# Transposes of x and o by DMA instead of TensorE, key features in half-height tiles, and a new order of each turn

## What is computed

```
q, k, v = heads(layernorm(x) @ Wq.T + bq), heads(ctx @ Wk.T + bk), heads(ctx @ Wv.T + bv)
qf, kf = relu(q @ Wqf.T), relu(k @ Wkf.T) * mask              # 64 features a head
kv, ksum = sum over keys of kf^T v, sum over keys of kf
x = x + (concat over heads of (qf @ kv) / (qf @ ksum + 1e-8)) @ Wo.T + bo
y = layernorm(x)
a = (quant(y) @ ternary(w_up).T) * relu(quant(y) @ ternary(w_gate).T) ** 2
x = x + quant(subln(a) * subln_weight) @ ternary(w_down).T
```

## Time and profile before

| what | value |
|---|---|
| median of 3 runs | 457.24 us (456.74 to 459.41) |
| profiled execution, its own time | 456.15 us |
| its span | 454.0 us |
| PE / DVE / ACT / POOL busy, share of the span | 90% / 85% / 73% / 32% |
| head | 0 to 31.0 us |
| turns 0, 1, 2, 3 | 63.0, 62.8, 60.9, 50.9 us |
| feed-forward | 185.5 us, from 268.6 us on |
| mean granted TensorE clock | 0.977 of full |

### The profile page before, as it was taken

One profiled execution on the slowest core, in us unless ns is written; L12 is line 12 of the kernel. 1 busy time (PEld: TensorE's weight loads), 2 busy tenths in 40 slices (PEclk: granted clock), 3 DMA queues, 4 the chain that ended last, 5 costly groups with the idle time before them and its releaser, 6 DMA issues. The chain is left out here.

```text
span 454.0 us, 8245 instructions
## 1 busy us (share of the span) xinstructions
PE 409.8 (90%) x2800; PEld 212.0 (47%) x2816; DVE 384.9 (85%) x822; ACT 331.7 (73%) x475; POOL 144.0 (32%) x146
## 2 busy tenths in 40 slices
PE   3997999999799998999994889899999989899955
PEld 1454546575255564455753634344444434344421
DVE  3588696699989998999889867999999999898962
ACT  5388998665667594866767658978788786988870
POOL 1018300046000821002200006646556464655430
PEclk9999999999899999999996799999999999999989
DMA  8899994001321242033111441333334342444234
GB/s 221 289 392 409 338 359 167 1 0 50 139 82 61 93 139 92 0 113 118 48 48 48 150 151 24 58 83 81 82 81 88 77 96 67 100 93 99 69 71 116
DMA packets 59025, 54.38 MB, mean 120 GB/s; under 512 B 45232, under 2 KB 45232, under 8 KB 58864
## 3 DMA queue, kind: packets, MB, share of 16 engines
q1 hardware_dynamic: 58096, 50.55, 36.9%
q0 software_dynamic: 896, 3.41, 2.0%
HBM read 39.27 MB, written 4.19 MB: 96 GB/s over the span
## 5 line engine op out<-in xcount | busy, mean ns | idle before, releaser
L1236 PE MATMUL ps<-tern,xqT 128*128 128x512 bf16 x503 | 112.5, 379 | 2.8 <-PEq L166 1.3
L1056 POOL TENSOR_TENSOR actg<-acts,subln 128x512 f32<-128x512 f32 x64 | 84.5, 1336 | 77.0 <-DVE acts L1139 72.3
L1236 PEld LDWEIGHTS ps<-tern,xqT 128*128 128x128 bf16 x512 | 49.6, 98 | 63.8 <-DVE acts L1139 3.8
L1249 PE MATMUL ps<-tern,aqT 128*128 128x512 bf16 x249 | 59.2, 387 | 12.1 <-DMA aqT<-aq 11.7
L1067 ACT ACTIVATE relu<-ps 128x512 f32<-128x512 f32 x64 | 37.3, 583 | 16.4 <-PE ps L1236 16.4
L1139 DVE TENSOR_TENSOR acts<-relu,ps 128x512 f32<-128x512 f32 x64 | 42.3, 678 | 4.4 <-ACT relu L1071 4.3
L1249 PEld LDWEIGHTS ps<-tern,aqT 128*128 128x128 bf16 x256 | 24.8, 99 | 45.2 <-DMA aqT<-aq 13.0
L1071 ACT ACTIVATE relu<-relu 128x512 f32<-128x512 f32 x64 | 40.3, 630 | 2.0
L537 DVE SCALAR_TENSOR_TENSOR fl<-ps,fh 128x512 f16<-128x512 f32 x64 | 39.6, 679 | 2.5 <-ACT fh L400 2.5
L1144 DVE TENSOR_REDUCE amax<-actg 128x1 f32<-128x1024 f32 x32 | 38.7, 1210 | 1.0 <-POOL actg L1056 0.7
L1078 ACT ACTIVATE square<-acts 128x2048 bf16<-128x2048 f32 x16 | 30.4, 1902 | 12.2 <-DVE acts L1139 12.2
(11 more groups left out here) (164 smaller groups left out, 963.6 us busy)
## 6 DMA issues: line engine op xcount, KB each, us to landing
tern<-in_wffn SPq DMA_DIRECT2D x24, 512.0 KB, 11.4
wst<-in_wffn SPq DMA_DIRECT2D x24, 512.0 KB, 3.2
xs<-in_x SPq DMA_DIRECT2D x4, 1024.0 KB, 7.4
out<-res SPq DMA_DIRECT2D x16, 256.0 KB, 2.2
ctxf<-in_ctxT POOLq DMA_DIRECT2D x3, 1024.0 KB, 10.1
xno<-in_wkT SPq DMA_DIRECT2D x4, 256.0 KB, 5.7
...
```

What stands on the lines that cost most here:

```text
L1056: nc.gpsimd.tensor_tensor(actg[:, s % 2, q], acts[:, s % 2, q], subln[:, q], ALU.mult)\
L1236: mm = nc.tensor.matmul(acc, xqT[:, s % XT, k, :], weights[k][:, 512 * c:512 * c + 512], start=(k == 0), stop=(k == KC - 1))
L1249: mm = nc.tensor.matmul(down_bank(s), aqT[:, s % 2, k, :], down_w[:, k, :], start=(k == 0), stop=(k == FK - 1))
```

## The change

- x and o are no longer transposed by PE. ACT makes the fp16 high half of the [128 x 512] tile (L549 of the changed kernel, L557 for o), POOL the low half beside it (L447, L454), and one DMA transpose on SP's queue turns the 1024 columns into `xT` or `oT` (L343, L350). `xn` is one buffer, `xn2`, `o32` and `o2` are two. ACT's normalising of tile n waits for POOL's low half of tile n-1, and its high half of tile n for the landing of transpose n-2.
- X and T leave `ORDER`, and `ORDER` is rewritten: F0 F1 Q0 F2 ... F7 Q1 Q2 S0 S1 S2 S3 Q3, K and V units spread between R, N and O.
- F uses 64*128 tiles: 96 matmuls of 128 columns a turn, alternating between the upper and the lower 64 rows, with two PSUM banks.
- POOL takes over the low half of kv (L460) and the clipping of the ternary chunks (L468). The context's load moves from POOL's queue to SP's, behind `ctx_split`.
- DVE's pieces for S and N are merged over two banks (fewer, wider instructions).
- The second group of x and its context are issued by SP ahead of the raw chunks; SP issues 6 raw chunks, then the four transposes of turn 0, then the other 18.
- All turns are written out (no hardware loop). `xqb` and `xqT` share the memory of the context.
- The feed-forward part is the same.

```diff
-ORDER = (
-    [("X", 0), ("X", 1)] + [("F", i) for i in range(4)] + [("X", 2), ("X", 3)] + [("F", i) for i in range(4, 8)]
-    + [("Q", 0), ("Q", 1), ("S", 0), ("S", 1), ("Q", 2), ("S", 2), ("S", 3), ("Q", 3)]
-    + [("R", p) for p in range(PAIRS)]
-    + [("K", m) for m in range(KC)]
...
+ORDER = [(u[0], int(u[1:])) for u in (
+    "F0 F1 Q0 F2 F3 F4 F5 F6 F7 Q1 Q2 "
+    "S0 S1 S2 S3 Q3 R0 R1 R2 R3 K0 R4 "
+    "R5 R6 R7 K1 V0 N0 N1 N2 N3 K2 N4 "
+    "N5 N6 N7 V1 V2 K3 O0 V3 O1 O2 O3 "
+).split()]
+ACT_AFTER = {
...
+    ("S", 1): (("norm", 0),),
...
+    ("N", 2): (("chunk", 2),),
+    ("N", 3): (("chunk", 3), ("oh", 0), ("norm", 2)),
...
# sync
+            for c in range(EARLY):
+                raw_chunk(c)
+            for t in range(GT):
+                turn_x(0, t)
+            for c in range(EARLY, NCH):
+                raw_chunk(c)
...
+            def turn_x(o, t):
...
+                if o > 0:
+                    sp.wait_ge(filled["Q"], o * KC)
+                sp.wait_ge(feat_ok, 1)
+                sp.wait_ge(xn_split, n + 1)
+                sp.dma_start_transpose(xT[:, :, t * P:t * P + P], xn2[:, n % 2, :]).then_inc(xT_in[n % 2], 16)
+            def turn_o(o, t):
...
+                sp.wait_ge(o_split, n + 1)
+                sp.dma_start_transpose(oT[:, :, t * P:t * P + P], o2[:, n % 2, :]).then_inc(oT_in[n % 2], 16)
# gpsimd
+                nc.gpsimd.tensor_tensor(xn2[:, n % 2, H:2 * H], xn[:, :], xn2[:, n % 2, 0:H], ALU.subtract)\
+                    .then_inc(xn_split, 1)
...
+                nc.gpsimd.tensor_scalar(ternh[:, c, :], wst[:, c % 2], 2.0, 1.0, ALU.min, ALU.subtract)\
+                    .then_inc(chunk_used, 1)
# scalar
+            def normalise(o, t):
...
+                if n > 0:
+                    act.wait_ge(xn_split, n)
+                nc.scalar.activation(xn[:, :], xs[:, n, :], ACT.Identity, bias=shift[:, t:t + 1],
+                                     scale=rstd[:, t:t + 1]).then_inc(xn_ok, 1)
+                if n > 1:
+                    act.wait_ge(xT_in[n % 2], landed(n - 2))
+                act.wait_ge(xn_ok, n + 1)
+                nc.scalar.activation(xn2[:, n % 2, 0:H], xn[:, :], ACT.Copy).then_inc(xn_high, 1)
# tensor
+                terms = ((qkTh, feath), (qkTl, feath), (qkTh, featl))
+                for c in range(KC):
+                    for n, (k, f) in enumerate(terms):
+                        for h in range(2):
+                            rows = slice(64 * h, 64 * h + 64)
...
+                            mm = nc.tensor.matmul(acc[:, c // 2, c % 2], k[rows, c, t * P:(t + 1) * P],
+                                                  f[rows, 0, P * h:P * h + P], start=(n == 0),
+                                                  stop=(n == len(terms) - 1))
```

783 lines of the change are left out of this document (403 added, 380 removed).

## The result

The changed kernel takes **472.97 us** (median of 4 runs, 470.94 to 477.23), the kernel before, on the same chip, 456.99 (455.45 to 459.41): a ratio of 1.036, 95% interval 1.027 to 1.044. The forecast was 448.2 with a range of 440 to 461, so it had the wrong sign and missed by 25 us. The profiled run took 472.07 us, 1.8 more than its span.

The account below looks back on a forecast made before the run. PE was taken to bind turns 1 and 2, DVE just behind; 454.0 + 13.5 - 9.8 - 7.9 - 4.9 = 444.9 us of span, 447.1 with 2.15 added, 448.2 as median; range 440 to 461.

Parts of the forecast that it names:

- eight clips 8 x 1.3 (L341 doubled): POOL's list in turns 1 and 2: each clip priced at 1.3 us, within 34.3 of 51 us busy.
- second rival: POOL's queue becomes the bound: at 2 us a clip o's later tiles come some 4 us late; 460 us, chance 13%.
- The chunks go round through POOL and back through SP: Turns 1 and 2: chunk 4 can be loaded once POOL has clipped chunk 2 at 29.7; ACT wants it at 34.
- The exclusive lock: VectorE and GpSimd share a pair of ports, locked for a whole instruction; the second rival's price was left as it was.
- Turn 0: the step: Turn 0: Q0 waits for four DMA transposes behind six raw chunks, starting at 50.2 instead of 41.8; 76.5 us, +13.5.
- fourth rival: Turn 0's transposes are not held by the raw chunks, so Q0 starts 7 us earlier; 441 us, chance 17%.
- first rival: F's row halves do not run side by side: +2.5 in turns 1 to 3; 455.7 us, chance 12%.
- third rival: A DMA transpose takes much longer than 3.2 us: gain gone at 5.6 us, 471 us at 8; chance 10%.
- Turns 1 to 3 with the assumed clip: Turns 1 and 2 at 53.0 us each (-9.8 and -7.9), turn 3 at 46 us (-4.9).
- the sum (25.4 to 32): Turn 3: all N done at 25.4, o's chain bare, its first transpose landed at 32, where O0 starts.

Follow-up runs that it names:

- a_clip_fast: The changed kernel with GpSimd's clip made a multiply by 1 and add of -1 over the same 1024 elements, clipping left out; 455.6 us, ratio 0.993 to 0.998.
- a_sign: The changed kernel with no clip on any engine: ScalarE's second pass over a chunk becomes a Sign written straight to bf16; 455.0 us, ratio 0.994 to 0.998.

## Why the prediction was wrong, point by point

- **The step that failed: "eight clips 8 x 1.3 (L341 doubled)".** L341 is a multiply and add of 512 elements, 658 ns. The clip is a min and subtract, and takes 3.66 us; multiply and add of 1024 takes 1.04. The same form of instruction on the same engine with other operations differs by 3.5 times. No row of before showed POOL doing a min or a scalar subtract; the price was taken from a row with the right form and the wrong operations. The runs showed in its place 29 us of clips a turn on POOL instead of 10.4, and a_clip_fast, with an instruction near the assumed duration in the same place (1.06 us), gives 455.6 us, inside the stated range.
- **The second rival, POOL's queue, was right as a mechanism and too cheap.** It was priced at 2 us a clip, 460 us, 13%. At 3.66 us POOL holds 29 us of clips and 24 of other work, in a turn of 60; the cost against 1.04 us was 17.3 us, where the rival had 12. What it lacked was SP, where two chunk loads stand ahead of o's first transpose and each waits for a clip, and kv's low half, which stood behind two clips in turn 1 (2.2 us on PE). The text had "The chunks go round through POOL and back through SP", but not that the transpose queues behind them.
- **The exclusive lock.** In the changed kernel three small instructions of VectorE ended within 0.03 us of POOL's additions of `bo`, and took 0.9 to 1.2 us each instead of 0.16. The Trainium skill, "SBUF — State Buffer", section "SBUF: two separate sides", has VectorE and GpSimd lock each other out for a whole instruction, where VectorE's has two inputs in SBUF or runs in a two-port mode. Those rows agree with it. Beside 3.8 us clips it is not so: VectorE's instructions of 512 and 1024 elements ran unchanged, a `TENSOR_TENSOR` with both inputs in SBUF took its 0.16 us (L682), and small ones were held at most 0.8. There the measurement decides. Leaving the lock out of the sum missed the longer chain ahead of R0 in turn 1: 2.6 us even with a quick clip.
- **Turn 0: the step was right, the sum 3.2 us short.** The sixth raw chunk landed at 40.5 (41.0 said), the first transpose at 41.4 (42.6), the last at 49.2 (50.2), Q0 ran from 49.34 to 54.54 (50.2 to 54.9). The sum let ScalarE's list start at Q0's end; but Q0's high half also waits for the last F (`filled_F` in its waits: it overwrites what F reads), and F2 to F7 take PE 2.0 us behind Q0:

```profile
56.79 0.69 ACT L525 ACTIVATE qkTh<-ps,bqk 128x512 f16<-128x512 f32 x1 [8.58 <-PE ps L849]
```

  From there to R7's high half it took 25.7 us (26 said), R7 was drained at 83.3 instead of 81.6, and PE waited for it until 83.5. Another 0.7 is O0's wait for `oT`, and the turn began 0.5 us earlier than before. R0's wait for the kv sums (2.0) lay beside ScalarE's list, which did not stop for it. That the transposes are not held, the fourth rival, fell: 9.1 us from the first issue, at 32.3, to its landing.
- **F's halves run side by side.** The 24 matmuls of F0 and F1 start within 0.63 us, a pair every 0.055, which is 2.7 us a turn where 2.6 were reckoned; the first rival fell. PE's first rows of turn 0:

```profile
30.56 0.23 PE L849 MATMUL ps<-feath,qkTh 64*128 64x128 f16 x2
30.63 0.22 PE L849 MATMUL ps<-feath,qkTl 64*128 64x128 f16 x2
30.68 0.22 PE L849 MATMUL ps<-featl,qkTh 64*128 64x128 f16 x2
```

- **The transposes take 3.0 to 3.8 us** to landing when little stands ahead of them; 3.2 was taken. The third rival, with its break-even at 5.6, fell, though its price for 8 us (471) came close to the result by another way.
- **Turns 1 to 3 with the assumed clip** are 56.6, 52.2 and 49.0, where 53.0, 53.0 and 46 stood: right in turn 2, 3.6 and 3.0 short in the others. In turn 1 R0 waits 2.6 us for the sums and the clock is 0.97. In turn 3 PE's wait for o ahead of O0, 5.9 us, was in the sum (25.4 to 32); but O0 started at 33.8, and a later tile made PE wait another 1.9 us inside O. With no clip at all (a_sign) O0 starts at 32.3, and the turn is 46.9.

With the clip's price and the turns of a_clip_fast put in, 448.2 + 17.3 (clip) + 3.5 (turn 0) + 3.6 (turn 1) - 0.8 (turn 2) + 3.0 (turn 3) = 474.8, against 473.0 measured. This is bookkeeping and no test: the terms are themselves measured. It shows the sizes, 17.3 us for the clip and 9.3 for all else.
